# Queries and keys written in f32 by ScalarE and split by GpSimd alone, with a planner fitted anew

## What is computed

```python
q = (x @ Wq.T + bq).reshape(B, T, HEADS, HEAD_DIM)
k = (keys @ Wk.T + bk).reshape(B, T + H, HEADS, HEAD_DIM)
v = (keys @ Wv.T + bv).reshape(B, T + H, HEADS, HEAD_DIM)
scores = jnp.einsum('bhqd,bhkd->bhqk', q, k) / jnp.sqrt(jnp.asarray(HEAD_DIM, x.dtype))
scores = jnp.where(valid[None, None], scores, neg)
attn = jax.nn.softmax(scores, axis=-1)
```

## Time and profile before

| | value |
|---|---|
| median of three runs | 1088.59 us |
| the profiled execution | 1091.71 us, its span 1089.9 us |
| PE busy | 992.6 us, 91% of the span |
| DVE busy | 803.6 us, 74% |
| ACT busy | 743.7 us, 68% |
| POOL busy | 394.4 us, 36% |
| mean granted clock of TensorE | 0.977 |

### The profile page before, as it was taken

The page is one execution under the profiler, slowest core; times in us unless marked ns, Lnnn a source line. Parts: engine busy times, 40 slices in busy tenths (PEclk is TensorE's granted clock), DMA queues, the critical chain, the costliest instruction groups (busy, mean ns, idle before and its releaser), DMA issues. The chain is left out here.

```text
span 1089.9 us, 47233 instructions
## 1 busy us (share of the span) xinstructions
PE 992.6 (91%) x20024; PEld 698.8 (64%) x20024; DVE 803.6 (74%) x2420; ACT 743.7 (68%) x1399; POOL 394.4 (36%) x528
## 2 busy tenths in 40 slices
PE   3689999999999999999998999999978988899996
PEld 2366767777766777777765776776656544455674
DVE  6877778777777788777788666768888889882321
ACT  6266766677767766766773777667767787888653
POOL 8311444332324443333344214324556364401211
PEclk9789999999999999999998999999999999999998
DMA  6721231322234221323224122112020311410220
GB/s 187 132 42 44 61 62 47 87 42 57 63 62 106 62 51 42 87 55 62 62 61 98 26 47 62 37 28 72 3 61 10 54 36 29 120 41 23 68 69 20
DMA packets 72626, 64.80 MB, mean 59 GB/s; under 512 B 16226, under 2 KB 66914, under 8 KB 72418
## 3 DMA queue, kind: packets, MB, share of 16 engines
q1 hardware_dynamic: 71554, 60.99, 23.9%
q10 hardware_dynamic: 864, 0.79, 0.4%
HBM read 15.70 MB, written 1.05 MB: 15 GB/s over the span
## 5 line engine op out<-in xcount | busy, mean ns | idle before, releaser
L1053 ACT ACTIVATE probs<-b 128x443 f32<-128x443 f32 (+2 forms) x736 | 356.5, 544 | 137.1 <-PE b L788 92.6
L1258 DVE TENSOR_REDUCE mx<-b 128x2 f32<-128x378 f32 (+1 forms) x768 | 351.8, 508 | 118.8 <-PE b L741 117.4
L708 PE MATMUL b<-band,identb 64*64 64x252 bf16 x2304 | 170.3, 285 | 18.1 <-DVE mx L1258 8.8
L807 PE MATMUL b<-probs,vals 128*32 128x189 f32 (+5 forms) x3968 | 177.3, 310 | 2.6 <-DVE mx L1255 1.3
L807 PEld LDWEIGHTS b<-probs,vals 128*32 128x32 f32 x3968 | 109.9, 110 | 53.2 <-issue 14.1
L788 PE MATMUL b<-qpack,kpack 64*64 64x189 bf16 (+5 forms) x3968 | 138.5, 235 | 4.4 <-issue 4.2
L1582 POOL TENSOR_SCALAR veps<-mv 128x4 f32<-128x4 f32 x48 | 11.0, 230 | 353.9 <-DVE mv L1364 353.6
L741 PE MATMUL b<-kpack,qpack 62*64 62x189 bf16 (+1 forms) x3072 | 123.9, 239 | 0.7 <-issue 0.7
L708 PEld LDWEIGHTS b<-band,identb 64*64 64x64 bf16 x2304 | 66.9, 105 | 79.3 <-issue 32.9
L919 PE MATMUL b<-w,hid 128*128 128x128 f32 x768 | 109.2, 286 | 1.1 <-DVE mx L1258 0.6
L1255 DVE TENSOR_REDUCE mx<-b 128x1 f32<-128x512 f32 (+7 forms) x256 | 99.3, 445 | 9.0 <-PE b L756 8.6
(11 more groups left out here) (174 smaller groups left out, 1650.8 us busy)
## 6 DMA issues: line engine op xcount, KB each, us to landing
qpack<-qparts SPq DMA_DIRECT2D x168, 128.0 KB, 3.6
kpack<-kparts SPq DMA_DIRECT2D x162, 128.2 KB, 3.6
qpack<-mrows SPq DMA_DIRECT2D x224, 4.0 KB
w<-in_w SPq DMA_DIRECT2D x12, 256.0 KB, 4.3
w<-in_wa SPq DMA_DIRECT2D x12, 256.0 KB, 2.8
w<-in_wb SPq DMA_DIRECT2D x12, 256.0 KB, 3.1
rowt<-in_rowt SPq DMA_DIRECT2D x6, 384.0 KB, 3.4
stream<-in_x SPq DMA_DIRECT2D x4, 256.0 KB, 4.4
```

The costliest lines, as they stand in the source:

```text
L708: pe.matmul(out, identb[rows, rows], rhs.unsqueeze(1).to_broadcast([64, 2, 2, EDGE]), start=True, stop=False, skip_group_check=True)
L807: mm = pe.matmul(bank("sum", u, group)[32 * j:32 * j + 32, q0:q0 + w - skip], vals[:, u % 2, at:at + 32], probs[:, n % SETS, j, col + skip ...
L1053: act.activation(probs[:, n % SETS, j, 0:width], bank("exp", u, v, b)[:, 0:width], ACT.Exp, scale=SCALE).then_inc(a_emptied, 1)
L1258: red = dve.tensor_reduce(out[:, 2 * tb:2 * tb + 2], read[:, 0:2 * width].rearrange("p (t k) -> p t k", k=width), AX.X, ALU.max)
```

## The change

ACT's copy of q or k now writes the sum of bank and bias in f32 into `qrest` or `krest` and frees the bank (the banks' semaphores move from DVE's to ACT's). It waits until unit u-1 is lowered, no longer until it is packed. DVE's `rests` is gone. POOL's `lower` waits for ACT's copy and for the packing of unit u-1, and then does four steps with a semaphore between each: cast to the high part, subtraction in place in f32, cast to the middle part, subtraction to the low part. The empty past key's column is computed once in a layer, as before.

The planner's costs are other numbers for many kinds of jobs (those of the q and k steps, and among others the statistics, scaling, roots, values, phase and GELU jobs). A PE job can't be planned to start sooner than RESTART = 170 ns after it is ready. A job that follows one of its own kind on its line has no lead after it. All priorities are other numbers. Of the new ones for PE's kinds in the layer loop: norm 1926401, turn 1817215, hid 1104808, q 0, score -4593, max -160096, out -167297, k -290161, cat -363790, v -1208817, parts -1261421, ffn -2764025, weigh -4610212. Of the old: turn 1328575, q 632237, cat 626734, norm 583361, hid 423046, k 15405, max 3452, v 3226, score 697, out -572133, parts -1284482, ffn -2325414, weigh -4423258.

```diff
 TURN = {"q": 200, "k": 200, "out": 205, "hid": 200, "ffn": 200, "mixin": 200, "mixv": 200, "ehid": 200, "eout": 200,
-        "cat": 152, "turn": 152, "norm": 152, "rows": 152, "weigh": 165, "v": 200, "phase": 200}
+        "cat": 152, "turn": 152, "norm": 152, "rows": 152, "weigh": 139, "v": 300, "phase": 200}
 TURN_LEAST, TABLE_LOAD = 122, 1400
+RESTART = 170
 FETCH, FETCHED, VLOADS = 3850, 256, 80
-TURN_WORTH = 827
-TABLE_WORTH = 188731
-SLACK = {"act": 323, "dve": 0, "pe": 23, "pool": 472, "sp": 953}
+TURN_WORTH = 171720
+TABLE_WORTH = 564044
+SLACK = {"act": 369, "dve": 0, "pe": 2, "pool": 0, "sp": 12194}
...
         after = [a for a in after if a is not None]
+        behind = self.last.get(line)
         if line is not None:
-            if line in self.last:
-                after.append(self.last[line])
+            if behind is not None:
+                after.append(behind)
             self.last[line] = name
         fills = takes if fills is None else fills
         self.jobs[name] = Job(engine, cost, after, tuple(takes), tuple(fills), tuple(frees), mode, landing)
+        self.jobs[name].queued = self.jobs[behind] if behind is not None and behind[0] == name[0] else None
 
     def nth(self, *name):
         return self.place[name]
@@ -185,6 +188,8 @@
         return self.earlier[key]
 
     def lead(self, source, job):
+        if source is job.queued:
+            return 0
         if source.engine == job.engine:
             return SAME[job.engine]
         return source.landing + LEAD[source.engine] + PULL[job.engine]
@@ -235,6 +240,11 @@
                         rooms = self.free[pool]
                         at = max(at, rooms[n - 1][0]) if len(rooms) >= n else math.inf
                     job.start = at
+                    ready = soon[name]
+                    for pool in {self.pool_of(k) for k in job.takes}:
+                        n = sum(self.pool_of(k) == pool for k in job.takes)
+                        ready = max(ready, self.free[pool][n - 1][0]) if len(self.free[pool]) >= n else ready
+                    job.ready = ready
                     if best is None or at < best[0]:
                         best = at, e
             at, e = best
@@ -254,6 +264,8 @@
             if job.mode is not None and mode[e] != job.mode:
                 at += TURN.get(name[0], TURN_LEAST) if e == "pe" else TABLE_LOAD
                 mode[e] = job.mode
+            if e == "pe":
+                at = max(at, job.ready + RESTART)
             job.start, job.end = at, at + job.cost
             if e == "pe":
                 n = fetched(name)
@@ -305,7 +317,7 @@
     kind = key[0]
     if kind == "sum":
         return "sum"
-    if kind in ("exp", "parts", "cat", "norm", "hid", "rows", "mixr", "router", "ehid"):
+    if kind in ("q", "k", "exp", "parts", "cat", "norm", "hid", "rows", "mixr", "router", "ehid"):
         return "act"
     if kind == "out":
         return "act" if causal(key[1]) else "dve"
@@ -320,45 +332,45 @@
     weights = ("load", l)
     for which in ("q", "k"):
         add("pe", (which, u), 862, [state, weights], takes=[(which, u)], mode=WIDE, line=which)
-        add("act", ("high", which, u), 618, [(which, u), ("pack", which, u - 1) if u else None], line="high" + which)
-        add("dve", ("rest", which, u), 670, [("high", which, u), ("lower", which, u - 1) if u else None],
-            frees=[(which, u)], line="rest" + which)
-        add("pool", ("lower", which, u), 1734, [("rest", which, u)], line="lower" + which)
+        add("act", ("high", which, u), 618, [(which, u), ("lower", which, u - 1) if u else None],
+            frees=[(which, u)], line="high" + which)
+        add("pool", ("lower", which, u), 3750, [("high", which, u), ("pack", which, u - 1) if u else None],
+            line="lower" + which)
         first = which == "k" and u == 0
-        add("act" if first else "sp", ("pack", which, u), 3900,
+        add("act" if first else "sp", ("pack", which, u), 4350,
             [("lower", which, u), ("score", u - BUFS, PAIRS // 2 - 1, banks_of(u - BUFS) - 1) if u >= BUFS
-             else (which + "clean", u)], line=None if first else "pack", landing=2500)
+             else (which + "clean", u)], line=None if first else "pack", landing=3000)
     if c:
-        add("pe", ("phase", u), 200, [state, ("later",)], takes=[("phase", u)], mode=HALF, line="phase")
-        add("dve", ("take", u), 2762, [("phase", u), ("open", u - 1) if u > UNITS else None], frees=[("phase", u)],
+        add("pe", ("phase", u), 850, [state, ("later",)], takes=[("phase", u)], mode=HALF, line="phase")
+        add("dve", ("take", u), 1900, [("phase", u), ("open", u - 1) if u > UNITS else None], frees=[("phase", u)],
             line="take")
-        add("pool", ("gates", u), 4630, [("take", u), ("sin",), ("consts",)], line="gates")
+        add("pool", ("gates", u), 5000, [("take", u), ("sin",), ("consts",)], line="gates")
         add("act", ("window", u), 160, [("gates", u)], mode="exp", line="window")
         add("pool", ("open", u), 1056, [("window", u), ("gated", u - 1) if u > UNITS else None], line="open")
         add("pe", ("v", u), 890, [state, weights], takes=[("v", u)], mode=HALF, line="v")
-        add("dve", ("gated", u), 1494, [("v", u), ("open", u), ("weigh", u - 2, 1, banks_of(u - 2) - 1)],
+        add("dve", ("gated", u), 1900, [("v", u), ("open", u), ("weigh", u - 2, 1, banks_of(u - 2) - 1)],
             frees=[("v", u)], line="values")
         values = ("gated", u)
     else:
         add("pe", ("v", u), 985, [state, weights, ("blank",)], takes=[("v", u), ("last", u)], mode=HALF, line="v")
         add("act", ("odd", u), 554, [("v", u), ("weigh", u - 2, 1, banks_of(u - 2) - 1) if u > 1 else ("blank",)],
             line="odd")
-        add("dve", ("even", u), 885, [("odd", u)], frees=[("v", u), ("last", u)], line="values")
+        add("dve", ("even", u), 1080, [("odd", u)], frees=[("v", u), ("last", u)], line="values")
         values = ("even", u)
...
-                add("act", ("gelu", u, f), 590, [("hid", u, f), ("ffn", u - 2, CHUNKS - 1) if u > 1 else None],
+                add("act", ("gelu", u, f), 460, [("hid", u, f), ("ffn", u - 2, CHUNKS - 1) if u > 1 else None],
...
-        add("dve", ("stats", u, ln), 1150, [("add", u, ln), ("root", u - 1, ln) if u else None], line=f"stats{ln}")
-        add("pool", ("root", u, ln), 1250, [("stats", u, ln), ("scale", u - 1, ln) if u else None], line=f"root{ln}")
-        add("dve", ("scale", u, ln), 1030, [("root", u, ln), ("norm", u - 1, ln) if u else None,
+        add("dve", ("stats", u, ln), 1265, [("add", u, ln), ("root", u - 1, ln) if u else None], line=f"stats{ln}")
+        add("pool", ("root", u, ln), 1355, [("stats", u, ln), ("scale", u - 1, ln) if u else None], line=f"root{ln}")
+        add("dve", ("scale", u, ln), 1200, [("root", u, ln), ("norm", u - 1, ln) if u else None,
...
+        q_left, k_left = sem("q_left"), sem("k_left")
...
-                          state[:, u % BATCH, 1:HEADED], start=True, stop=True).then_inc(d_filled, 1)
+                          state[:, u % BATCH, 1:HEADED], start=True, stop=True).then_inc(a_filled, 1)
...
             def high(u, name):
                 par, first = weights_of(u), 0 if name == "q" else 1
-                parts, done, packed = (qparts, q_hi, q_packed) if name == "q" else (kparts, k_hi, k_packed)
+                full, lo = (qrest, q_lo) if name == "q" else (krest, k_lo)
                 column = COL_BQ if name == "q" else COL_BK
                 bias = cols[:, par, column:column + 1]
                 act.wait_ge(w_loaded[par], loaded(u))
                 if u:
-                    act.wait_ge(packed, u * PACKED)
-                act.wait_ge(d_filled, filled(name, u))
+                    act.wait_ge(lo, u)
+                act.wait_ge(a_filled, filled(name, u))
                 if name == "k" and u % BATCH == 0:
-                    act.activation(kparts[:, 0, 0:1], zero[:, :], ACT.Identity, bias=bias).then_inc(past_ready, 1)
-                act.activation(parts[:, 0, first:], bank(name, u)[:, :], ACT.Identity, bias=bias
-                               ).then_inc(done, 1)
+                    act.activation(krest[:, 0:1], zero[:, :], ACT.Identity, bias=bias).then_inc(past_ready, 1)
+                act.activation(full[:, first:], bank(name, u)[:, :], ACT.Identity, bias=bias).then_inc(a_emptied, 1)
 
-            def rests(u, name):
-                rest, parts_, hi, lo = (qrest, qparts, q_hi, q_lo) if name == "q" else (krest, kparts, k_hi, k_lo)
-                first, column = (0, COL_BQ) if name == "q" else (1, COL_BK)
-                bias = cols[:, weights_of(u), column:column + 1]
-                if u:
-                    dve.wait_ge(lo, u)
-                dve.wait_ge(hi, u + 1)
-                if name == "k" and u % BATCH == 0:
-                    dve.wait_ge(past_ready, u // BATCH + 1)
```

(62 more changed lines are left out.)

19 lines of the change are left out of this document (8 added, 11 removed).

## The result

The changed kernel takes 1086.49 us (median of 20 runs, 1083.28 to 1089.98), the kernel before 1090.49 us in 20 runs beside them. The ratio is 0.9963, with a 95% interval of 0.9948 to 0.9977: faster by 4 us, a third of the 12 that were forecast. The profiled execution took 1086.9 us, its span 1085.1 us.

A forecast was written before the change was run, and what follows sets the result against it. PE was taken as the bound in the loop and experts, shared with DVE in 770:953. Terms -4 - 3 - 3 - 3 + 1 = -12 us from the median 1088.6 gave 1076.6, say 1076 us; range 1057 to 1099.

The forecast's parts named there:

- Where PE is bound: PE bounds the layer loop (95 to 770 us, 648.0 of 675 busy) and the experts (125.3 of 127).
- I cost that at 0 in the sum, since the cover is there: POOL takes over the packing-DMA wait; layer-norm roots queue behind it, covered by other units' maxima on DVE: 0 us.
- the shared access at 1 us: A few DVE instructions wait out a POOL instruction, nearly all under PE's cover: +1 us, between 0 and 8.
- Rival (c): Slower: roots wait behind POOL's longer pieces; 1110 uncovered, 1097 half covered; decided by DVE's root wait passing 30; chance 0.18.
- DVE's 42 us: DVE's subtraction goes: 28 q and 28 k instructions of 0.75 us, eight of the 56 in 770:953.
- start -4: ACT no longer held in 33:62: 6.5 of 11 us PE idle won, less 2.5 for later first maxima.
- middle -3: 95:770, 27 us of PE idle: banks freed earlier and 36 us less on DVE take part, between 0 and 10.
- 770:953 -3: Last loop units and causal attention: 6 us less on DVE against 16.5 more on POOL; between -7 and +3.
- The fitted order: Planner fitted anew: 25 turns of PE's tile shape fewer of 876, at 0.12 us: -3 us, bounds +10 and -13.
- rival (a): Nothing net: PE is bound, waits move, the start loses what it wins, turns stay; 1087 us, chance 0.30.
- The port rule: DVE and GpSimd's shared ports lock for a whole instruction, so DVE gets back part of its 42 us as waits.
- The signs of being wrong: First exponential near 60, PE's waits behind norm chains growing, or PE's busy time moving by more than 5 us.

The follow-up runs named there:

- old_order_short: The change's code in the kernel before's order, GpSimd's f32 subtraction and second cast left out from unit 1 on: 1085.36 us, 0.9928 of the kernel before.
- short_lower: The changed kernel in its own order, GpSimd's f32 subtraction and second cast left out from unit 1 on: 1069.18 us, 0.9792 of the kernel before.
- tiny_instead: The changed kernel's order, two 128x4 power instructions replacing GpSimd's f32 subtraction and second cast from unit 1 on: 1078.76 us, 0.9871 of the kernel before.

## Why the prediction was right or wrong

*Where PE is bound* was right: in the changed kernel PE is 98% busy in the loop and 99% in the experts. What the change wins it wins in the loop, and most of what it loses it loses from 770 to 953, where DVE and PE share the bound.

*"I cost that at 0 in the sum, since the cover is there"* is the step that failed: GpSimd's longer piece, with its queue at nothing and the shared access at 1 us. It costs 18 us in the new order and 50 in the old. Its time itself was sized well (100 us more, 116 forecast). Rival (c) named this mechanism and its mark: with DVE's wait for the root at 49.7 us in the old order, past the mark of 30, the kernel is 43 us slower than before. In the new order the wait is 18.5 and the kernel faster. What I failed to see is that the old order could not carry the longer piece. In the new list nearly as many roots stand directly behind a piece (19 for 20), but only 2 start within 0.4 us of its end, where the old order with the same code has 18: the new order keeps them apart in time.

*DVE's 42 us, ACT's bf16 to f32, the banks* (start -4, middle -3, 770:953 -3, together -10): in the old order with the short piece they measure -8. In 0:95 PE is busy 2.8 us more, against 4 forecast, with the first maxima 3.2 us late (2.5 taken). ACT's copy costs the same, 0.685 us.

*The fitted order*: I took 25 turns fewer, -3 us; there are 24 more. Yet with the short piece in both the new order is worth 15 to 16 us (`old_order_short` to `short_lower`), and with the long one 49 (1135.7 to 1086.5). By counting turns I looked at the wrong thing; PE's idle time in the loop went from 27 to 13 us.

*The sum as the runs give it*: code -8, order -15 or -16, longer piece +17 to +19, which makes -4 to -7; forecast were -10, -3 and +1. Two large terms were missed and nearly cancel. That the time fell inside the range, and close to rival (a)'s 1087, is luck: (a) expected that next to nothing moves.

*770:953, -3*: here about 12 us are lost against the lead at 770, nearly all of it by 850. The bound that I gave, +3, was too near. DVE had been named as sharing the bound, and 16 us more on POOL stood in the text, but the packs and roots before the causal units were not followed to the engine that waits for them.

*The port rule.* The Trainium skill's "SBUF — State Buffer", section "SBUF: two separate sides", has it right for the scaling beside casts and subtractions of 128x512: four tensor_scalar instructions took 3.73 us beside the pieces and 1.12 when they went first. The power instruction on 128x4 departs from that rule: three scalings ran beside it in 0.34 us each, so there the measurement decides. The maxima aren't touched: 542 ns median, 540 before. The warning that such a move might not help, in the Trainium skill's "Perfetto Trace Analysis", section "Optimizing Scalar/DVE Operations", names no size. Here DVE got back 9 to 13 of its 42 us as longer instructions (775.1 us busy, against 765.8 and 762.6 us in `tiny_instead` and `short_lower`), 17 were forecast; what was wrong is that they are nearly all covered: they cost 8 to 10 us of the kernel's time.

*The signs of being wrong.* PE's busy time moved by more than 5 us (992.6 to 1000.8), "which only turns can do". 24 turns at 0.12 make only 3; the mean clock fell from 0.977 to 0.971, 13 us more at the lower level, which can lengthen PE's work by up to 6 (an estimate). PE's idle time in 770:953 was to fall below 23 us and is 29.7.

The direction was right; the chance of 0.46 for a gain over 1% stood too high against 0.35 for no change.

## What to carry to other kernels

Work moved to an engine that is busy a third of the time is not hidden by that: look in its list for what stands behind the moved work, follow that to the engine that waits, and price it where two engines already share the bound. A longer piece on an in-order queue and the order of that queue are one change: here the new code in the old order was 43 us slower, and the new order with that code 49 us faster. Where two engines share access, try letting the short work of the one go first: here it brought 5 to 8 us at three places.

## What the runs showed of the hardware

- GpSimd's power instruction on 128x4 takes 1.01 us and hardly delays DVE (four scalings in 1.43 us beside two of them), while beside a cast (0.61 us) or subtraction (1.16 us) of 128x512 each DVE tensor_scalar of 128x128 lasts until GpSimd's instruction ends (0.63 to 1.33 us in place of 0.34). So how long GpSimd is busy doesn't decide; whether the small operand or the kind of operation does wasn't separated.
- A GpSimd subtraction of 128x512 takes 1.16 us with an f32 or a bf16 output (1.159 and 1.160), while the sum of two f32 operands of that size takes 1.29.
- Between 20 runs of the changed kernel the time goes up by 0.24 us for each microsecond at the clock's lower level (correlation -0.93 of mean clock and time).
